# Rewriting the second attention of a two-layer vision tower: strips of 64 rows, scores in both orientations, values held stationary by quarters, class tokens inside each image

## The reference

```python
qkv = src @ in_proj_w.T + in_proj_b                       # src: layernorm of h, (8, 257, 256)
q, k, v = split(qkv)                                      # 16 heads of 16 features
attn = softmax(q @ k.T / sqrt(16));  ctx = attn @ v
dense_output = ctx @ out_proj_w.T + out_proj_b
Q = src @ Qp_w.T + Qp_b; K = src @ Kp_w.T + Kp_b; V = src @ Vp_w.T + Vp_b      # Q, K: 64 features
aw = softmax(Q @ K.T / sqrt(64))
topv, topi = top_k(aw, 51)                                # the 51 largest of 257 are kept, rescaled
sparse_output = renormalised(aw kept) @ V
fused = sig * dense_output + (1 - sig) * sparse_output    # sig = sigmoid(lam)
x = layernorm(src + fused)                                # then a feed-forward block
```

## Time and profile before

| | us |
|---|---|
| median of 3 runs (1581.98 to 1585.31) | 1582.93 |
| own time of the profiled execution | 1581.55 |
| its span, first to last instruction | 1579.8 |
| `fused_attention`, first instruction to last (604.5 to 1239.4) | 634.9 |
| of it: before the first sparse score / eight images / class tokens at the end | 53.5 / 496 / 85.4 |
| TensorE busy over the span; mean granted clock | 79%; 0.852 of 2.4 GHz |
| VectorE, ScalarE, GpSimd busy over the span | 54%, 30%, 30% |

### The profile page before, as it was taken

The page is one execution under the profiler, slowest core; times in us unless marked ns, Lnnn a source line. Parts: engine busy times, 40 slices in busy tenths (PEclk is TensorE's granted clock), DMA queues, the critical chain, the costliest instruction groups (busy, mean ns, idle before and its releaser), DMA issues. The chain is left out here.

```text
span 1579.8 us, 24346 instructions
## 1 busy us (share of the span) xinstructions
PE 1253.3 (79%) x7331; PEld 990.6 (63%) x7331; DVE 849.7 (54%) x1986; ACT 474.1 (30%) x1404; POOL 472.1 (30%) x662
## 2 busy tenths in 40 slices
PE   0368878615999902899998998999999699869888
PEld 0357766513777601477777777777979599746555
DVE  8956661311222243266775775777640178668885
ACT  0323330101222201244554554455310245322221
POOL 5930100152000063112112111121130277546665
PEclk9979996557999955589998998999575699979999
DMA  5034000122111130000000000000000300000000
GB/s 203 2 101 139 0 0 1 61 72 71 59 59 59 50 98 15 0 1 1 1 1 1 1 0 1 0 1 1 1 1 0 128 1 0 0 1 7 13 13 21
DMA packets 36443, 46.94 MB, mean 30 GB/s; under 512 B 4432, under 2 KB 32896, under 8 KB 36224
## 3 DMA queue, kind: packets, MB, share of 16 engines
q1 hardware_dynamic: 33152, 37.47, 7.2%
q0 software_dynamic: 3200, 8.43, 1.7%
HBM read 29.08 MB, written 16.80 MB: 29 GB/s over the span
## 5 line engine op out<-in xcount | busy, mean ns | idle before, releaser
L2003 PE MATMUL fa_ps<-fa_v,fa_pt 128*128 (+2 forms) x1088 | 158.9, 281 | 0.0
L2003 PEld LDWEIGHTS fa_ps<-fa_v,fa_pt 128*128 128x128 f32 x1088 | 156.7, 216 | 3.3
L1636 ACT ACTIVATE fa_e<-fa_ps,fa_nm 128x257 f32<-128x257 f32 x272 | 126.4, 473 | 98.5 <-DVE fa_nm L1814 97.1
L1522 POOL COPY fa_e<-fa_e 128x2 f32<-128x2 f32 x128 | 24.5, 192 | 377.2 <-ACT fa_e L1636 323.4
L1927 PE MATMUL fa_ps<-fa_xT,wf_qk 128*128 128x257 f32 (+1 forms) x320 | 104.7, 456 | 24.0 <-DVE fa_vc L1696 9.0
L1814 DVE TENSOR_REDUCE fa_nm<-fa_ps 128x2 f32<-128x514 f32 x136 | 93.7, 689 | 53.5 <-PE fa_ps L1955 41.6
L1290 PE MATMUL ex_ps<-we_raw,ex_xT 128*128 x320 | 118.3, 493 | 0.0
L1982 PE MATMUL fa_ps<-ident,fa_e 128*128 128x128 f32 x512 | 90.8, 305 | 3.8 <-ACT fa_e L1636 3.3
L2677 PE MATMUL qf_ps<-qf_wg,qf_xT 128*128 128x352 f32 x272 | 89.7, 479 | 2.1 <-ACT qf_xT L2518 1.4
L1084 POOL DMA_INDIRECT ex_got<-y_rows,ex_pos_i x34 | 32.1, 943 | 196.9 <-DMA y_rows<-ex_y 186.9
L1927 PEld LDWEIGHTS fa_ps<-fa_xT,wf_qk 128*128 128x128 f32 (+1 forms) x320 | 58.3, 204 | 51.0 <-DVE fa_vc L1696 12.1
(11 more groups left out here) (418 smaller groups left out, 2748.1 us busy)
## 6 DMA issues: line engine op xcount, KB each, us to landing
we_raw<-in_L_ffn_W SPq DMA_DIRECT2D x24, 384.0 KB, 8.0
x_rows<-tk_zero SPq DMA_DIRECT2D x1, 5120.0 KB, 19.4
ex_xin<-x_rows SPq DMA_DIRECT2D x40, 128.0 KB
y_rows<-ex_y SPq DMA_DIRECT2D x40, 128.0 KB, 1.7
wq_raw<-in_ffn_rows SPq DMA_DIRECT2D x1, 2240.0 KB, 14.6
wg_f<-in_ff SPq DMA_DIRECT2D x2, 1024.0 KB, 8.4
out<-h SPq DMA_DIRECT2D x8, 256.0 KB
tk_c<-in_x SPq DMA_DIRECT2D x1, 1024.0 KB, 4.9
```

Source lines behind the costliest of these rows:

```text
L1636: last = cp(dst, ps[:, SB + 2 * par + t, 0:TOK], ACT.Exp, bias=nm[:, par, t:t + 1], accum_out=sums[:, p, sl, t:t + 1])
L2003: last = mm(dst, pt[:, par, c, t * P:(t + 1) * P], rhs, start=(c == 0), stop=(c == 1))
```

## The change

`fused_attention` is written anew; the rest of the program is the same but for a `shift` that takes ranges, and some semaphores that live longer. In it, for each image `u` (front steps are made for `u + 1` while `u` is worked on):

- The queries and keys are projected without padding (2 + 2 matmul groups of 128 features in place of 4 + 4), split in high and low parts by VectorE (`high_parts`) and GpSimd (`low_parts`), written to DRAM by two DMAs (`strips_out`) and read back by eight (`strips_in`), each of which fills 16 partitions: a head then lies in 64 rows, all four products of high and low in one matmul.
- Scores are made twice: once in the old orientation for the row maxima (`head_scores`, of image `u + 1`, in slots 8 to 15), and, when the maxima have been turned and brought by DMA into rows 64 and 65 of the query strips (`max_rows`), once with the keys stationary (`turned_scores`), so that the exponentials come out turned, with the maximum already subtracted. The transposes of the probabilities and their copies fall away.
- The context is made with the values stationary, 32 columns per head (16 values and a one for the sum), four heads side by side in the four column quarters of the array (`quad`), over 256 moving columns.
- The row sums go by DMA to DRAM and back (`sums_out`, `sums_in`), VectorE inverts them (`shares`), and by DMA again out and back, spread over 32 rows each (`shares_out`, `shares_in`); GpSimd scales the context (`shared_context`), and the projection takes context, sparse part and class value in one accumulation (`project`).
- Class tokens are a column of each image (`class_query`, `class_keys`, `class_context`); only their top-k and the sparse product stay behind the last image.

The orders on the queues that the prediction speaks of, and the DMAs:

```diff
+            def strips_out(u, p, part, low, out, read):
+                sp.wait_ge(z[low], u + 1)
+                ...
+                sp.dma_start(d["fa_qk"][part, p].rearrange("b r n -> r b n"), src[:, :, :, :].rearrange("r a c n -> r (a c) n")
+                             ).then_inc(z[out], 16)
+            def strips_in(u, p, part, out, read):
+                sp.wait_ge(z[out], 16 * (u + 1))
+                ...
+                for i in range(4):
+                    a = i % 2 if part == 0 else i // 2
+                    sp.dma_start(dst[DH * i:DH * (i + 1), p, :, 0:TOK].bitcast(F32),
+                                 src[KC * a:KC * (a + 1)].rearrange("c (h d) n -> d (c h) n", d=DH)).then_inc(z[read], 16)
+            def sums_out(u, p):
+                sp.wait_ge(z["clsq_taken"], u + 1)
+                sp.wait_ge(z["cx_taken"], QUADS * (u + 1))
+            def shares_in(u):
+                sp.wait_ge(z["rs_out"], 16 * (u + 1))
+                ...
+                sp.dma_start(rsb[:, :, :].rearrange("p c n -> p (c n)"),
+                             d["fa_rs"].unsqueeze(1).broadcast_to([4, STRIP, QUADS * TOKP])).then_inc(z["rsb_in"], 16)
+            def body(u, p, first, more):                      # SyncE
+                max_rows(u, p, 1)
+                if not first:
+                    sums_out(u - 1, 1 - p)
+                if more:
+                    class_values(u + 1, 1 - p)
+                if not first:
+                    sums_in(u - 1)
+                if more:
+                    strips_out(u + 1, 1 - p, 0, "ql_ready", "q_out", "q_in")
+                    strips_out(u + 1, 1 - p, 1, "kl_ready", "k_out", "k_in")
+                if not first:
+                    shares_out(u - 1)
+                if more:
+                    strips_in(u + 1, 1 - p, 0, "q_out", "q_in")
+                    strips_in(u + 1, 1 - p, 1, "k_out", "k_in")
+                if not first:
+                    shares_in(u - 1)
+                ...
+    ROUNDS_AT = {0: 2, 1: 2, 2: 2, 3: 1, 4: 2, 5: 2, 6: 2, 7: 1}
+    HEADS_AT = {8: (0,), 9: (1, 2), 10: (3, 4), 11: (5, 6), 12: (7, 8), 13: (9, 10), 14: (11, 12), 15: (13, 14, 15)}
+            def head_scores(u, p, j):                         # TensorE
+                if j == 0:
+                    pe.wait_ge(z["q_in"], 64 * (u + 1))
+                    pe.wait_ge(z["k_in"], 64 * (u + 1))
+                ...
+                b = SB + 2 * ((j + 1) % 2)
+                for t in range(2):
+                    last = mm(ps[:, b + t, 0:WID], qs[0:ROWS, p, j, 1 + t * P:1 + (t + 1) * P], ks[0:ROWS, p, j, :],
+                              start=True, stop=True)
+            def turned_scores(u, p, j):
+                ...
+                for c in range(2):
+                    last = mm(ps[:, ST + j % 2, c * SEQ:(c + 1) * SEQ], ks[0:ROWS + 2, p, j, 1 + c * P:1 + (c + 1) * P],
+                              qs[0:ROWS + 2, p, j, 1:TOK], start=True, stop=True)
+            def quad(u, p, c):
+                ...
+                mm(ps[:, CB, cols], vblk[:, p, 4 * c:4 * c + 4, :], e0T[:, p, 0:SEQ], start=True, stop=False)
+                for k in range(2):
+                    for j in range(4):
+                        last = mm(ps[STRIP * j:STRIP * (j + 1), CB, cols], v[:, p, k, 4 * c + j, :],
+                                  eT[:, (4 * c + j) % 8, k * SEQ:(k + 1) * SEQ], start=False, stop=(k == 1))
+            def body(u, p, first, more):
+                for sl in range(16):
+                    turned_scores(u, p, sl)
+                    if sl == 0:
+                        if more:
+                            turn_rows(u + 1)
+                        turn_maxima(u, 1, more)
+                    if sl == 1:
+                        class_keys(u)
+                        if more:
+                            queries_keys(u + 1)
+                    if sl == 2 and not first:
+                        quad(u - 1, 1 - p, 3)
+                    if sl == 3 and more:
+                        sparse_operands(u + 1)
+                    if sl == 3 and not first:
+                        class_context(u - 1, 1 - p)
+                    if sl == 5:
+                        quad(u, p, 0)
+                    if sl == 7 and more:
+                        class_query(u + 1)
+                    if sl == 9:
+                        quad(u, p, 1)
+                    if sl == 10 and more:
+                        turn_class_probs(u + 1)
+                    if sl == 11 and not first:
+                        project(u - 1, 1 - p, more)
+                    if sl == 12:
+                        turn_weights(u, first)
+                    if sl == 13:
+                        quad(u, p, 2)
+                        turn_class_weights(u)
+                    if sl == 14 and more:
+                        turn_maxima(u + 1, 0, True)
+                    if more:
+                        for j in HEADS_AT.get(sl, ()):
+                            head_scores(u + 1, 1 - p, j)
+                    if sl == 15 and more:
+                        values(u + 1, 0)
+                        values(u + 1, 1)
+                        sparse_scores(u + 1)
```

More of the change, by code:

```diff
@@ L1440, in _ @@
+            sums_out(BATCH - 1, 1)
+            sums_in(BATCH - 1)
+            shares_out(BATCH - 1)
+            shares_in(BATCH - 1)
             sp.wait_ge(z["fetched"], 16 * len(loads))
@@ L1558, in _ @@
+            step(g.tensor_copy(vblk[:, 1, :, DH], ident[0:NH, 0:NH]))
+            low_maxima(0, 0)
+            low_maxima(0, 1)
+            class_values(0, 0)
+            pipelined(pool, BATCH, body)
+            shared_context(BATCH - 1, 1)
         @block.scalar
@@ new lines, in turn_weights @@
+            def turn_weights(u, first):
+                pe.wait_ge(z["wk_ready"], 2 * u + 2)
+                if first:
+                    pe.wait_ge(z["pt_taken"], 2)
+                else:
+                    pe.wait_ge(z["z_added"], u)
+                for c in range(2):
+                    for t in range(2):
+                        last = nc.tensor.transpose(ps[:, FB, (c * 2 + t) * P:(c * 2 + t + 1) * P],
+                                                   WK[:, t, 1 + c * P:1 + (c + 1) * P], ident[:, :])
+                last.then_inc(z["wt_ps"], 1)
@@ L1903, in _ @@
+            pe.wait_ge(z["xnc_ready"], 1)
             for k in range(KC):
@@ new lines, in _ @@
+            values(0, 0)
+            values(0, 1)
+            sparse_scores(0)
+            pe.wait_ge(z["sbo_ready"], 1)
+            pe.wait_ge(z["vc_ready"], 2)
+            pipelined(pe, BATCH, body)
+            quad(BATCH - 1, 1, 3)
+            class_context(BATCH - 1, 1)
+            pe.wait_ge(z["wkc_ready"], 1)
+            for c in range(2):
+                last = nc.tensor.transpose(ps[:, SB, c * BATCH:(c + 1) * BATCH], WKc[:, 1 + c * P:1 + (c + 1) * P],
+                                           ident[0:BATCH, 0:BATCH])
@@ new lines, in _ @@
+            last.then_inc(z["wct_ps"], 1)
+            pe.wait_ge(z["wcm_ready"], 1)
+            pe.wait_ge(z["v2_in"], 16)
+            pe.wait_ge(z["e_ready"], N * BATCH)
+            for b in range(BATCH):
+                for c in range(2):
+                    mm(ps[0:BATCH, ST, 0:SEQ], wcm[:, c, b, :], v2all[:, b, c, :], start=(b + c == 0), stop=False)
+            mm(ps[0:BATCH, ST, 0:SEQ], d8[:, :], vc8[:, SEQ:2 * SEQ], start=False, stop=False)
+            project(BATCH - 1, 1, False, done=True)
@@ L2091, in _ @@
+            pe.wait_ge(z["cc_ready"], BATCH)
+            for c in range(QUADS):
+                last = mm(ps[0:BATCH, ST, 0:SEQ], ccT[:, c, :], w["o"][:, c, :], start=False, stop=(c == QUADS - 1))
             last.then_inc(z["yc_ps"], 1)
```

1283 lines of the change are left out of this document (691 added, 592 removed).

## The result

| us | before | predicted | after |
|---|---|---|---|
| median of the runs | 1584.12 (4 runs) | 1519 (1440 to 1630) | 1699.95 (4 runs, 1698.08 to 1707.09) |
| span of the profiled execution | 1579.8 | | 1696.3 |
| mean granted clock of TensorE | 0.852 | | 0.771 |

The change makes the kernel slower: the ratio is 1.0738, with a 95% interval of 1.0701 to 1.0775. I had given "slower" 0.23.

What follows compares the result with a forecast made beforehand. TensorE was taken to set the pace, at 62 us per image. Opening 51, image 0 50, six images of 64, last image and end 83 and semaphores 3.5 gave a 571.5 us stage for 634.9, so 1519 us (1440 to 1630).

Steps and rivals of the forecast that it cites:

- step 2: SyncE's queue per image: sums, then strips out and in; the eight loads take 5.5 us and land at A + 13.
- step 3: TensorE stands at the first head score from 21 to 29.5 us, a new wait of 8 us per image.
- time 0: Start of the count for one image: the moment its sparse exponentials are done.
- second rival: Loads into 16 partitions get a quarter of 386 GB/s: 16.3 us more, images at 80, total 1641; chance 0.22.
- the nearest row: Trace row that priced the strip transfers: the store of x_rows, 386 GB/s in 1 KB pieces.
- step 6: TensorE's clock falls to half after two idle times per image, 5 us each, 2.6 lost each, 5.2 in both.
- B: Part of an image behind the strip wait, from head scores through `project` to sparse scores: 26 us.
- the boundary: Between images: sparse maximum and exponentials 1.7 us, jump back 1.5 us on average.
- third rival: TensorE slower: quads in sequence +8.6, clock +8, total 1570; or `shares_in` on a quarter of engines, +25; chance 0.13.
- A: Time of `take_class` in an image, when SyncE's queue moves on: 16.5 us.
- The rest of the last image: Sums of image 6, its projection, then weights and quads, before the class tokens' end: 45 us.
- first rival: Strips are there in time, so an image is work and boundary, 50 us; total 1433; chance 0.2.

Runs made afterwards that it cites:

- e4b: Changed kernel with 40 added 256-column matmuls in TensorE's queue ahead of its strip wait, in images 1 to 7: 1692.84 us.
- e8: Changed kernel with one pass pair in place of the 72 one-column passes of `class_context`: 1680.0 us.
- e10: e9 with `turn_weights` of slot 12 moved behind that slot's head scores: 1597.6 us, 1.0094 of the kernel before.
- e12: e10 with `shares_in` ahead of all strip loads on SyncE and a memset of ones moved later: 1576.5 us, 0.9955 of the kernel before.
- e7: Changed kernel with strip loads to every fourth partition, head scores from slot 11, `shares_in` between strip loads, and `strips_out` ahead of `sums_out`: 1649.68 us.
- e14: Changed kernel with `shares_in` as four DMAs in place of one and nothing else: 1695.22 us.
- e9: e7 with `shares_in` as four DMAs, one for each quarter of the partitions: 1605.84 us.
- e5: Changed kernel with the first head score in slot 11 instead of 8, and `shares_in` between query and key strip loads: 1724.12 us.
- e11: e9 with the first head score back in slot 8, as in the changed kernel: 1637.96 us.
- e3: Changed kernel with each strip load going to every fourth partition of 64 instead of 16 neighbouring ones: 1648.77 us.
- e2: Changed kernel with each strip load going to 128 partitions instead of 16, same bytes and rows: 1637.15 us.

## Why the prediction was wrong

**The step that failed first: step 2, the rate of the strip loads.** I priced 2105 KB at 386 GB/s, from stores of x_rows, and got 5.5 us; they run at 117 and take 20. The wait of TensorE (step 3) was 18.3 us for 8, and its head scores began 43.3 us after time 0 for 29.5: 13.8 us per image. That was my second rival, by its own mechanism and nearly its numbers (16.3 more, images at 80). The reason I gave against it, that all 16 engines take part, is true and says nothing: the page shows them busy at a share of 1.04 to 1.16 while they move a third. And "the nearest row" was no near row. It was a store, spread over 128 partitions, used for a load into 16. A price had to be bounded by how far the row is off in the thing that differs.

**The second: step 6, the clock.** I allowed 5.2 us per image, 2.6 behind each of two idle times. Measured are 64.1 us of busy time for 41 us of work at full clock, so 23 us, of which some 4 (slots 4 to 7) lie ahead of the strip wait and are hidden in it. B took 43.4 us for 26 (954.1 to 997.5). Of the terms: the strip wait costs some 4 us of busy time behind it (e4b, mean of six images), more than my 2.6 and less than the 6.5 that 13 us at half clock lose, as before showed at a loop's jump; the one-column passes of `class_context` take the clock down with no idle time (e8); and it falls again around slots 12 and 13, behind a 1.4 us idle time (after) and also where 0.7 us are left (e10). This last fall stays open: neither the passes there nor the short idle time was taken away whole. Once down, the clock came up, but for one case, only in three places of an image (e12 above); step 6 let it come up 5 us behind each idle time, whatever stands there. My third rival had 8 us per image more for the clock, where 12 came, and I gave it 0.13 because I looked only for idle times, not for what kind of work stands between them.

The two together: 13.8 + (43.4 - 26 - 5.2 = 12.2) is 26 for the 24.2 that an image is off; the image read here is 0.8 us longer than the mean of six, and the boundary's 1.7 and 1.5 were 1 to 2 us too much.

**What was right.** TensorE's work (43 for 41 to 42 us), the quads side by side (1.07 us for 16 passes), A (927.7 - 910.8 = 16.9 for 16.5), the order of SyncE's queue as the thing that decides (e7, e12), the end of the class tokens (1317 to 1354, 37 us for 38; L2335 in 9.7 for 9 to 10), the semaphores. Image 0 (+17.8) and the opening (+9.5, a strip wait of 18.0 us in it) are off by the same two steps.

**`shares_in`.** The clause of the third rival was right in mechanism (share 0.25, 97 to 103 GB/s, about the 5.6 us) and wrong in place: in the images it is hidden behind the strips (e14). It cost some 5 us in the last image, and 6 us per image as soon as the heads were moved (e9). That `project` would be the next to wait I had seen for the shares but not for the move of the heads, which is why e5 missed.

**The rest of the last image** was 55 us for 45: the 10.6 us at `project`.

**The ranges.** Forecast and rival differed in one unknown price, and the rival's price was an estimate worked out as a quarter of a rate. With the clock's term it came to 1700 for its 1641, outside the range, because I treated a slow transfer and a low clock as separate cases, though the wait brings a low clock with it (e4b). One sum was off besides: the terms of the first rival give 1434 against the profile and 1436 against the median, for its 1433.

## What to carry to other kernels

A transfer's price goes by the partitions that it reaches as well as by its bytes: spreading a tile's rows over the partitions (one index in a slice) was worth 51 us here, and no busy share of the engines gives the slowness away, only share and GB/s read together. When a wait is taken off a queue's head, ask which transfer the next waiting instruction needs: moving the head scores later cost 24 us while the shares landed last (e5), and was worth 32 once they landed sooner (e9 against e11). Work counted at full clock is a lower bound; a design of many small, thin passes has to be priced with the clock of the rows that look like it.

## What the runs showed of the hardware that I had not expected

- 16 neighbouring partitions 117 GB/s, 16 partitions four apart 190 to 201, 128 partitions 352 to 376, with the same bytes, rows and count of loads (after, e3, e2).
- The clock was 1.00 before 72 passes of one column and 0.50 some 1 us behind them, TensorE being busy throughout; with these left out it stayed at 1.00 (e8).
- In e4b the 80 added 256-column passes, behind 8 us of work at half clock, ran 5.5 us more at half clock before it rose (20.14 us for all), and the 64-row head scores behind them held full clock for 5 us; behind 1.4 us of idle time it was half again. In e12 the clock stayed at 0.50 through 20 us of work without a break (882 to 902).
- The loads into every fourth partition take SyncE longer to issue: 2.49 to 2.76 us for four (e3), against 1.81 to 1.97 into neighbouring ones (after).
- A memset of two partitions of 8256 elements took 6.94 us on VectorE, one of 128 partitions of 1024 elements 0.91.
